# Second attention of a two-layer graph network: from one tile per step to four tiles per step

## The reference

```python
src = concatenate([edge_index[0], loops]); dst = concatenate([edge_index[1], loops])
xp = (x @ W).reshape(n, H, C)                      # H = 4 heads, C = 64
a_src = einsum('nhc,hc->nh', xp, att_src)
a_dst = einsum('nhc,hc->nh', xp, att_dst)
alpha = leaky_relu(a_src[src] + a_dst[dst], negative_slope=0.2)
amax = segment_max(alpha, dst, num_segments=n)
ex = exp(alpha - amax[dst])
w = ex / segment_sum(ex, dst, num_segments=n)[dst]
agg = segment_sum(xp[src] * w[..., None], dst, num_segments=n)
out = elu(agg.reshape(n, H * C) + bias)
```

## Time and profile before

| | |
|---|---|
| median of the runs | 4472.5 us |
| span of the profiled execution, first to last instruction | 6181.0 us |
| first gather of the first attention | 350.72 us |
| last gather of the first attention issued | 3278.58 us |
| first gather of the second attention | 3359.56 us |
| last gather of the second attention issued | 6124.04 us |
| granted TensorE clock, first attention / second | 0.94 / 0.61 |
| DVE, ACT busy in the second attention | 1457.93, 1256.60 of 2764 us |

### The profile page before, as it was taken

The page is one execution under the profiler, slowest core; times in us unless marked ns, Lnnn a source line. Parts: engine busy times, 40 slices in busy tenths (PEclk is TensorE's granted clock), DMA queues, the critical chain, the costliest instruction groups (busy, mean ns, idle before and its releaser), DMA issues. The chain is left out here.

```text
span 6181.0 us, 164556 instructions
## 1 busy us (share of the span) xinstructions
PE 4261.5 (69%) x50798; PEld 2746.6 (44%) x50798; DVE 3295.8 (53%) x10527; ACT 2576.2 (42%) x6781; POOL 3049.7 (49%) x3229
## 2 busy tenths in 40 slices
PE   7958878777778787778786555555555555555554
PEld 4634444444444444444443444444444443444443
DVE  3235555555555555555554455555555555555555
ACT  2323344444444444444343444444444444444444
POOL 1245555545555555555452555555555555555553
PEclk9989999999999999999997666656566566565666
DMA  7856676666666666666664555555555555555554
GB/s 224 282 163 191 185 189 186 186 186 185 186 187 183 186 186 187 185 186 186 184 185 114 145 153 156 152 151 153 152 153 153 150 152 149 154 152 152 154 150 123
DMA packets 820553, 1055.91 MB, mean 171 GB/s; under 512 B 458633, under 2 KB 632338, under 8 KB 820464
## 3 DMA queue, kind: packets, MB, share of 16 engines
q0 software_dynamic: 225072, 730.03, 42.9%
q1 hardware_dynamic: 594078, 324.02, 20.6%
q10 hardware_dynamic: 1314, 0.99, 0.1%
HBM read 919.46 MB, written 133.59 MB: 170 GB/s over the span
## 5 line engine op out<-in xcount | busy, mean ns | idle before, releaser
L766 POOL DMA_INDIRECT typed_rows<-kv,typed_index x1563 | 1491.3, 954 | 1470.8 <-remote 570.5
L1298 POOL DMA_INDIRECT plain_rows<-xp,plain_index x1563 | 1486.0, 951 | 1359.5 <-remote 536.1
L875 PE MATMUL typed_p_s<-typed_kt,typed_q 64*32 64x416 f32 x4168 | 835.7, 549 | 336.6 <-issue 289.7
L997 DVE CUSTOM_DVE_ANT_0 typed_weight<-typed_p_s,typed_far 128x416 f32<-128x416 f32 x521 | 308.3, 592 | 1113.6 <-PE typed_p_s L875 1080.8
L1400 PE MATMUL plain_p_o<-plain_rows,plain_weight_t 128*32 128x65 f32 x16672 | 630.5, 296 | 331.5 <-issue 310.7
L1433 DVE SCALAR_TENSOR_TENSOR plain_p_s<-plain_p_s,plain_a_dst,plain_damped 128x416 f32<-128x416 f32 x521 | 342.3, 657 | 865.9 <-ACT plain_damped L1553 475.1
L1389 PE MATMUL plain_p_s<-all_cst,plain_rows 128*128 128x128 f32 x2084 | 546.2, 395 | 346.0 <-issue 319.6
L1375 PE MATMUL plain_p_w<-all_cst,plain_weight 128*128 128x128 f32 x1563 | 437.5, 404 | 431.6 <-issue 286.0
L1400 PEld LDWEIGHTS plain_p_o<-plain_rows,plain_weight_t 128*32 128x32 f32 x16672 | 459.2, 154 | 556.6 <-issue 516.7
L1167 ACT ACTIVATE typed_weight<-typed_weight,typed_col 128x416 f32<-128x416 f32 x521 | 334.7, 642 | 806.6 <-issue 549.7
L1389 PEld LDWEIGHTS plain_p_s<-all_cst,plain_rows 128*128 128x128 f32 x2084 | 406.0, 210 | 463.6 <-issue 437.6
(11 more groups left out here) (191 smaller groups left out, 6936.5 us busy)
## 6 DMA issues: line engine op xcount, KB each, us to landing
typed_match<-match SPq DMA_DIRECT2D x131, 208.0 KB
plain_match<-match SPq DMA_DIRECT2D x131, 208.0 KB
agg<-qkv_zero SPq DMA_DIRECT2D x98, 264.0 KB
typed_agg<-agg SPq DMA_DIRECT2D x98, 264.0 KB
plain_agg<-agg SPq DMA_DIRECT2D x98, 264.0 KB
kv<-qkv_kv SPq DMA_DIRECT2D x98, 258.0 KB
typed_kinds<-match SPq DMA_DIRECT2D x131, 192.0 KB
typed_rows<-kv,typed_index POOLq DMA_INDIRECT x1563
```

Source lines behind the costliest of these rows:

```text
L766: pool.indirect_dma_start(rows[:, r, j, :], None, k.kv, bass.IndirectOffsetOnAxis(ap=index[:, g, at:at + 1], axis=0)).then_inc(rows_in[r], 16)
L875: last = pe.matmul(p_s[at:at + TN, 0:SLOTS], q[own, m, :, h // 2], kt[own, h // 2, lo:lo + SLOTS], start=True, stop=True, tile_position=(H ...
L1298: pool.indirect_dma_start(rows[:, r, j, :], None, k.xp, bass.IndirectOffsetOnAxis(ap=index[:, g, at:at + 1], axis=0)).then_inc(rows_in[r], 16)
```

## The change

`attend_plain` is rewritten to take a batch of four tiles per step (`by_batch`, 131 batches, the last of one tile). The other stages keep their code, but for the row that `copy_row` builds: the 128 columns of repeated scores go, and a row of `xp` has 268 floats (1072 bytes).

- A batch's scores stand per edge and not per node: `p_a` is 128 x 64, partition = edge in the chunk, columns = 4 chunks (the last 32 slots) x 4 tiles x 4 heads. PE adds the target score through a 0/1 matrix (`home`, 128 x 416, made by DVE) and the source score through the identity.
- Node maxima come from two prefix scans on 16 partitions (tile and head) x 416 slots, with `fresh` marking where a new node begins (`find_tops`). PE turns the scores before and the maxima after.
- `mark_nodes` makes the 0/1 matrix `one` (128 x 512) of the batch, `spread_weights` multiplies it by the weights of the four heads into `spread` (128 x 2048); `aggregate` uses its 32-column pieces as the stationary side, four tiles side by side.
- ACT only takes the exponential of 128 x 64 and copies 128 x 264 sums out. Indices are copied from SBUF by DVE.
- The ring `rows` holds 3 batches. The gather of batch b waits until batch b - 3 has been aggregated. The number of gathers (1563) stays.
- Before the first batch a setup turns the place codes into the layout per edge.

The core of the diff:

```diff
-V1 = VW + P + 2 * HEADS
+V1 = VW + 2 * HEADS
...
+            def gather(b):
+                r, g = b.slot(RB), b.slot(AHEAD_INDEX)
+                if not b.known_below(RB):
+                    pool.wait_ge(agg_done, b.n - RB + 1)
+                pool.wait_ge(index_ready, b.n + 1)
                 pool.sem_inc(settled, 1)
-                for j in range(CH):
-                    at = b * CH + j
-                    pool.indirect_dma_start(rows[:, r, j, :], None, k.xp, bass.IndirectOffsetOnAxis(
-                        ap=index[:, g, at:at + 1], axis=0)).then_inc(rows_in[r], 16)
+                for i in range(tiles_of(b)):
+                    for j in range(CH):
+                        at = i * CH + j
+                        pool.indirect_dma_start(rows[:, r, i, j, :], None, k.xp, bass.IndirectOffsetOnAxis(
+                            ap=index[:, g, at:at + 1], axis=0)).then_inc(rest_in[r] if i else rows_in[r], 16)
...
+            def add_scores(b):
+                pe.wait_ge(home_ready, b.n + 1)
...
+                if not last_batch:
+                    pe.wait_ge(rest_in[r], b.use(RB) * (16 * CH * (TPB - 1)) + 16 * CH * (TPB - 1))
+                    later = b.back(-1)
+                    pe.wait_ge(rows_in[later.slot(RB)], later.use(RB) * (16 * CH) + 16 * CH)
...
+                for j in range(CH):
+                    at = j * LANES
+                    pe.matmul(p_a[:, at:at + LANES], home[:, j * P:j * P + P], a_dst[:, m], start=True, stop=False, skip_group_check=True)
+                    pe.matmul(p_a[:, at:at + LANES], ident, rows[:, r, :, j, A_SRC:A_DST], start=False, stop=True, skip_group_check=True)
...
+            by_batch(pe, PE_FIRST, PE_UNROLL, BatchPart(1, add_scores), BatchPart(1, turn_scores), BatchPart(2, aggregate), BatchPart(1, turn_tops))
...
+            def find_tops(b):
...
+                v.tensor_tensor_scan(running[0:LANES], fresh[0:LANES, m, 0:SLOTS], p_s[0:LANES, 0:SLOTS], -3.0e38, ALU.add, ALU.max).then_inc(running_ready, 1)
...
+                v.tensor_tensor_scan(top[0:LANES, ::-1], fresh[0:LANES, m, 1:SLOTS + 1][:, ::-1], running[0:LANES, ::-1], -3.0e38,
+                                     ALU.add, ALU.max).then_inc(top_ready, 1)
+
+            def mark_nodes(b):
+                if not b.known_below(1):
+                    v.wait_ge(agg_done, b.n)
+                v.tensor_tensor(one[:].rearrange("p (e i) n -> p e i n", i=TPB),
+                                cst[:, C_LINE:C_LINE + TN].unsqueeze(1).unsqueeze(1).broadcast_to((P, EDGES, TPB, TN)),
+                                by_edge(code, b).unsqueeze(3).broadcast_to((P, EDGES, TPB, TN)), ALU.is_equal).then_inc(one_ready, 1)
...
+            def spread_weights(b):
+                v.wait_ge(exp_done, b.n + 1)
+                v.wait_ge(one_ready, b.n + 1)
+                v.tensor_tensor(spread[:], one[:].unsqueeze(2).broadcast_to((P, EDGES * TPB, HEADS, TN)),
+                                weight[:].rearrange("p (e h) -> p e h", h=HEADS).unsqueeze(3).broadcast_to((P, EDGES * TPB, HEADS, TN)),
+                                ALU.mult).then_inc(spread_ready, 1)
```

More of the change, by code:

```diff
@@ L306, in interleave, with __init__, end, at @@
         step(Step(0, n, PERIOD))
+class BatchPart:
+    def __init__(self, lag, fn):
+        self.lag, self.fn = lag, fn
+    def end(self):
+        return BATCHES + self.lag
+    def at(self, t):
+        if not isinstance(t.q, int):
+            self.fn(t.back(self.lag))
+        elif 0 <= t.n - self.lag < BATCHES:
+            self.fn(Step(0, t.n - self.lag, t.unroll))
+class NodePart:
+    def __init__(self, shift, fn):
+        self.shift, self.fn = shift, fn
+    def end(self):
+        return block_place(ROWS - 1) // TPB + self.shift + 1
+    def at(self, t):
+        rel = t.c - self.shift - POS // TPB
+        if rel % CYCLE >= GROUP:
+            return
+        b = Step(t.q, GROUP * (rel // CYCLE) + rel % CYCLE, GROUP)
+        if not isinstance(t.q, int):
+            assert b.c >= 1
+            self.fn(b)
+        elif 0 <= b.n < ROWS:
+            self.fn(b)
+def by_batch(eng, first, unroll, *parts):
+    assert (BATCHES - first) % unroll == 0
+    def step(t):
+        for part in parts:
+            part.at(t)
+    for n in range(first):
+        step(Step(0, n, unroll))
+    with eng.Fori(0, (BATCHES - first) // unroll) as q:
+        for c in range(first, first + unroll):
+            step(Step(q, c, unroll))
+    for n in range(BATCHES, max(part.end() for part in parts)):
+        step(Step(0, n, unroll))
+def tiles_of(b):
+    return LAST if isinstance(b.q, int) and b.n == BATCHES - 1 else TPB
 def group_of(t):
@@ new lines, in fetch @@
+            def fetch(b):
+                m = b.slot(MB)
+                nodes = nodes_of(b, places)
+                if not b.known_below(MB):
+                    sp.wait_ge(top_ready, b.n - MB + 1)
+                    sp.sem_inc(slot_free, 1)
+                tiles = bass.ds(b.n * TPB, TPB)
+                sp.dma_start(match[:, m], k.match[1, tiles].unsqueeze(1).broadcast_to((TPB, TN, SLOTS))).then_inc(match_in[m], 16)
+                for i in range(TPB):
+                    with nc.allow_non_contiguous_dma(reason="four values per node"):
+                        sp.dma_start(a_dst[TN * i:TN * i + TN, m, HEADS * i:HEADS * i + HEADS],
+                                     k.xp[bass.ds(nodes[i], TN), A_DST:V1]).then_inc(a_dst_in[m], 16)
+                sp.dma_start(fresh[0:LANES, m], k.fresh[tiles].unsqueeze(1).broadcast_to((TPB, HEADS, SLOTS + 1))).then_inc(fresh_in[m], 16)
```

434 lines of the change are left out of this document (232 added, 202 removed).

## The result

The changed kernel takes 5005.5 us (median of 4 runs, 5003.6 to 5010.1), the kernel before 4471.9 on the same chip: ratio 1.119, 95% interval 1.118 to 1.121. It is 534 us slower. The forecast was 4775 with a range of 4420 to 5060. Direction and first cause were right, and 260 us of the size came from a wait that I had priced at 0. The time lies inside the range, but outside the 4660 to 4900 that I gave this mechanism by itself: the range holds it because it was drawn wide enough for the rivals.

The account below looks back on a forecast made before the run. The prediction took GpSimd's nearly unbroken gather issue, 1.25 us each, as the bound in both attentions. From 4472.5 us, +308 for the held port, 0 for the ring and -6 at the start gave 4775, range 4420 to 5060.

Parts of the forecast that it names:

- GpSimd bounds the runs at 1.25 us a gather: Both attentions: GpSimd issues 1563 gathers each almost without a break, 1954 us per attention, assuming 1.25 holds without the profiler.
- The third rival: Second attention: a gather takes 1.0 us in the runs, so saved work counts; 105 us less, about 4365; chance 0.16.
- The held port: Second attention: new VectorE instructions with two SBUF inputs lengthen GpSimd's gathers; 2.35 us per batch, 308 us (283 to 333).
- The two moments: A two-SBUF-input instruction lengthens a gather when it covers its start or about 0.45 us later; L1594's mean loss 1.79 us.
- The scan: Second scan, L1572 on DVE: one or two cycles a column, loss 0.15 or 0.53 us a batch, middle 0.34 taken.
- The ring: Gather of batch b waits for the sums of b - 3: no wait on average, 0 us, bounds 0 and +1.5 (+200).
- T + 11: When GpSimd may go on after the sums of b; T is the landing of the first tile of b+2.
- First rival, ring late: PE keeps half its profiled stops in the runs: 19 to 20.5 us a batch, +530 to +720, about 5100; chance 0.12.
- Ends: Second attention: the 5.79 us wait at the start goes, -6; behind the last gather 57 us stays, bounds -15 and +25.
- The profiled span: Profiled execution, where PE's stops count: 21.7 us a batch against 21.3, span from 6181 to 6230 (6100 to 6450).

Follow-up runs that it names:

- the repaired kernel: The changed kernel with a ring of four batches and three operands (`weight`, constants of `one`, first scan's result) in PSUM: 4501.0 us, ratio 1.006.
- the twin runs: One unread 128x2048 product per four tiles added to the kernel before: 4665.2 us with both inputs in SBUF, 4514.5 with one in PSUM.
- added product: The kernel before with one unread 128x2048 VectorE product per four tiles, both inputs in SBUF: 4665.2 us, ratio 1.043.
- the operands in PSUM: The changed kernel, ring still three deep, with `weight`, the constants of `one` and the first scan's result in PSUM: 4717.9 us, ratio 1.055.
- the last order: The repaired kernel with two gathers a tile, `finish` moved ahead of `one` and `join` behind the scans in VectorE's order: 4188.8 us, ratio 0.936.

## Why the prediction was right, and where it was not

- **GpSimd bounds the runs at 1.25 us a gather.** Right. Undisturbed gathers start every 1.25 us in the profile after as well; the kernel before with fewer gathers is 4% faster; the repaired kernel comes back to 4501. The third rival (1.0 us in the runs) is out.
- **The held port, 2.35 us a batch, 308 us.** That there is such a hold is shown by the twin runs and by `weight` in PSUM. The size was 2.07 with the ring of three and 1.82 with four batches: 270 and 237 us. Of the 2.07, `spread` has 1.78, the second scan 0.24, node parts and `home` 0.05, and `one` nothing, as no gather starts under it. `spread` takes 2.29 us (2.2 to 2.3 forecast), and all gathers of 2 us and more start under L1594.
- **The two moments.** This reading of the trace was wrong: only one moment counts, the gather's start. In the profile of before all 59 gathers of 1.0 us and more start while a VectorE instruction with all its inputs in SBUF runs; 116 times one began only behind a gather's start and covered the moment 0.45 us after it, and every one of these gathers took 0.95 us. One of them:

```profile
3505.54 0.95 POOL L1298 DMA_INDIRECT plain_rows<-xp,plain_index  x1 [0.30 <-issue]
3505.91 0.43 DVE L1452 TENSOR_TENSOR plain_both<-plain_agg 128x264 f32<-128x264 f32 x1
```

With one moment the mean over all phases is, by an estimate from the measured lengths, 1.5 us for `spread` (a gather starting w behind it lasts 2.29 + 0.82 - w, so 2.16 - w more, with w from 0 to 1.25), 0.1 for `one` and 0.3 for the scan: 1.9 a batch, or 250 us, and not 2.35. The added product, of the same length, lengthened gathers by 1.41 us itself. The phases aren't free, though: in 93 of 128 batches of the changed kernel a gather starts within 0.3 us behind `spread` and loses 2.0 us, in 35 it starts 0.8 to 1.0 us behind it and loses 1.3.
- **The scan.** 1.012 us for 416 columns. L1594 and L1578 take 2292 and 692 ns for 2048 and 512 columns, 1.04 ns a column and 0.16 us beside; by this the scan needs 2.0 ns a column. That agrees with the half throughput that the Trainium skill gives ("DVE: opcode table, instruction layouts, handler registers and perf-mode slots", "Datapath and trigger behaviour"); I had taken the middle. The gather of 3511.33 above, beside L1572, took 1.53 us, 0.58 more.
- **The ring: 0 us.** Wrong, and this is the step that failed: "GpSimd finishes batch b+2 at T + 9.25, with the holds T + 11.5", just over the T + 11 at which the aggregation lets it go on. The T + 11 was exact: first score to aggregation's end 10.16 us and 0.92 to the next gather, together 11.08. But I put the whole 2.35 of holds on the nine gathers behind T. In fact the first three, ahead of T, last 5.28 us instead of 3.45, which leaves 0.24 for the nine; and a landing took 2.71 us, not 2.3. So GpSimd is done at T - 2.71 + 0.30 + 11.25 + 0.24 = T + 9.1, and waits 2.0 us, 260 us in all. My bound of +1.5 was too low. The loop closes to the number: 5.28 + 2.71 + 10.16 + 0.92 = 19.07 us, against 19.08 measured; with the operands in PSUM 3.44 + 2.28 + 10.16 + 0.92 = 16.80, against 16.91 (here a wait of 17 us at the start of the stage is spread over the batches). For the profiled execution I had seen that `spread` falls just then; I didn't carry it over to the runs.
- **The two causes are one in part.** Each edit alone gives back nearly the same: 296 us the ring, 283 the operand. Together it is 504, less than their sum 579, as the hold in the first three gathers costs a wait of the ring's too.
- **First rival, ring late.** Its 19 to 20.5 us a batch and +530 to +720 hold the measured 19.08 and +534; the forecast's own 17.35 and +303 lie well under them. It named the ring, but with PE's stops of the profiled execution as its cause, and these are not in the profile after. Its place was right, its reason wrong.
- **Ends: -6.** The end behind the last gather grew from 57 to 69.5 us: +13, inside the bounds. The start gave nothing: the wait of 5.79 us after 24 gathers is absent from the profiles with the added product, so the runs of before had none to lose. In the changed kernel the first 36 gathers follow each other without a wait, as forecast (2448.74 to 2493.04 us), but then the ring is full and GpSimd stands for 17 us, since the first aggregation comes only behind the setup. With a ring of four no wait over 2 us stands there. POOL of the changed kernel:

```profile
2493.04 0.95 POOL L1386 DMA_INDIRECT plain_rows<-xp,plain_index  x1 [0.30 <-issue]
2511.18 0.94 POOL L1386 DMA_INDIRECT plain_rows<-xp,plain_index  x1 [17.19 <-PE plain_p_o L1524]
```

- **The profiled span, 6230.** Wrong: 5002.2. The stops aren't a property of this kernel's profile, and kernels made from the one before show none either (4661.9 of span for a run of 4665.2). What caused them in the profile of before stays open.

## What to carry to other kernels

When GpSimd issues DMAs back to back, a DMA issue that starts under a long VectorE instruction with two SBUF inputs waits for its end; with one operand in PSUM none here waited for it. When two engines are released by the same event, don't average over their phases: they meet at the same one or two places each time, here mostly near the worst. Ask, too, whether the lost time lies inside the loop that the ring closes. Before a saving on an idle engine is counted, take away the bound by itself (fewer gathers) and see what comes next; here it was the order in VectorE's queue.

## What the runs showed of the hardware

- A gather that starts under a long VectorE instruction with both inputs in SBUF ends 0.81 to 0.84 us after the instruction's end, wherever it began (some 385 gathers under `spread` or the added product, in the changed kernel, with the ring of four and in the run with both inputs in SBUF): 3519.55 against 3518.73 in the changed kernel, 3508.52 against 3507.70 with the added product. Behind the scan it is 0.76. One that has started before the instruction isn't held: in the same three traces `spread` or the product began behind a gather's start and covered the moment 0.45 us after it 114 times, and all these gathers took 0.95.
- The rule of the Trainium skill ("SBUF — State Buffer", "Who interferes with whom"), that a VectorE instruction with two SBUF inputs contends with what GpSimd reads, holds for an instruction whose hold is some eight times the longest in the profile of before (0.26 us). Its probe, in which `tensor_tensor` didn't stop DMAs issued by GpSimd, does not describe these indirect gathers.
- A stage whose TensorE is busy 1294 of 2480 us ran at 1.2 GHz throughout; the same stage filled with idle matmuls was granted 0.80 of full speed. The kernel before, with two gathers a tile, had 0.84 with 921 of 1600 us busy (2700 to 4300 us); the repaired one in the last order had 0.50 with 1097 of 1400 (2700 to 4100 us). The busy share of a whole stage doesn't tell its clock.
